# Three PSUM copies of a feed-forward stage go from the vector engine to ScalarE, and a tanh recurrence is dealt out anew

## The reference, cut to what matters

```
# layer 0, feed-forward
h = bit_linear(x, w1)                      # 256 -> 1024, quantized x and ternary weights
h = silu(depthwise_conv1d(h, conv_w, 3 taps) + conv_b)
h = bit_linear(h, w2)                      # 1024 -> 256: max over a token, scale, round, multiply
# layer 1, recurrence, 1024 steps that depend on each other
Bu = x @ B_w.T + B_b
state = tanh(state * exp(A) + Bu[:, t])    # 64 states, 4 sequences
y = states @ C_w.T + C_b + (x @ D_w.T + D_b)
```

## Time and profile before

| | us |
|---|---|
| median of 3 runs (2614.31 to 2617.99) | 2614.32 |
| the profiled execution, its own time | 2614.64 |
| its span, first to last instruction | 2612.9 |
| `ffn0`: first silu to last silu, 31 slots | 1135.75 to 1558.86 |
| `ffn0` with steps: from silu of slot 7 to the last | 1213.17 to 1558.86 |
| `keys` stage | 1591.4 to 1659.1 |
| `values` stage | 1659.9 to 1731.3 |
| `cross_layer1` | 1731.9 to 2189.3 |

### The profile page before, as it was taken

One profiled execution on the slowest core, in us unless ns is written; L12 is line 12 of the kernel. 1 busy time (PEld: TensorE's weight loads), 2 busy tenths in 40 slices (PEclk: granted clock), 3 DMA queues, 4 the chain that ended last, 5 costly groups with the idle time before them and its releaser, 6 DMA issues. The chain is left out here.

```text
span 2612.9 us, 35515 instructions
## 1 busy us (share of the span) xinstructions
PE 1856.3 (71%) x11685; PEld 1177.5 (45%) x11696; DVE 1883.8 (72%) x4634; ACT 1337.4 (51%) x3303; POOL 802.5 (31%) x889
## 2 busy tenths in 40 slices
PE   8759999999478888844554446668999995444444
PEld 4413333333267767733443333345667773222222
DVE  4678888884478888868888883335666664888886
ACT  2106666667033334415999998977742221233332
POOL 3500000000054364323333320004435533444442
PEclk9959999999599999967666765678999997666665
DMA  2011111110200000000000001000000000000000
GB/s 71 16 32 27 31 29 30 30 28 7 55 13 11 29 11 11 3 1 1 1 1 1 1 1 51 13 17 1 17 1 1 1 1 30 7 13 11 10 13 15
DMA packets 42805, 41.50 MB, mean 16 GB/s; under 512 B 16054, under 2 KB 34670, under 8 KB 42622
## 3 DMA queue, kind: packets, MB, share of 16 engines
q1 hardware_dynamic: 42622, 39.23, 5.6%
HBM read 22.03 MB, written 4.19 MB: 10 GB/s over the span
## 5 line engine op out<-in xcount | busy, mean ns | idle before, releaser
L763 ACT ACTIVATE ST<-ST,aexp 128x1 f32<-128x1 f32 x2046 | 574.7, 374 | 11.6 <-PEq L57 11.6
L597 ACT ACTIVATE PT<-PS 128x512 f32<-128x512 f32 x576 | 309.8, 597 | 219.4 <-PE PS L482 188.5
L94 PE MATMUL PS<-ident,j_t 128*128 128x128 f32 x320 | 84.9, 431 | 233.9 <-DVE j_t L155 156.7
L558 DVE CUSTOM_DVE_ANT_0 junk<-PS,maskw 128x128 bf16<-128x128 f32 (+3 forms) x512 | 226.5, 486 | 33.8 <-PE PS L459 33.8
L459 PE MATMUL PS<-KT,QT 48*128 48x512 bf16 (+3 forms) x768 | 190.4, 351 | 54.1 <-DMA QT<-QS 33.0
L94 PE MATMUL PS<-ident,X 128*128 128x128 f32 x320 | 76.2, 325 | 212.6 <-DVE X L128 195.3
L561 DVE TENSOR_REDUCE MX<-PS 128x1 f32<-128x512 f32 x256 | 164.6, 685 | 27.7 <-PE PS L459 24.8
L501 PE MATMUL PS<-PT,VP 128*32 128x256 f32 (+1 forms) x2560 | 184.2, 370 | 0.0
L94 PEld LDWEIGHTS PS<-ident,j_t 128*128 128x128 f32 x320 | 59.4, 219 | 259.2 <-DVE j_t L155 169.0
L123 POOL TENSOR_TENSOR n_rs<-n_ve,neghalf 128x1 f32<-128x1 f32 x96 | 110.3, 1165 | 208.0 <-DVE n_ve L118 208.0
L1561 PE MATMUL PS<-L_xattn_VW,l_pT 112*128 112x256 f32 x704 | 161.4, 385 | 9.1 <-DVE i_xb L1587 6.3
(11 more groups left out here) (297 smaller groups left out, 4471.0 us busy)
## 6 DMA issues: line engine op xcount, KB each, us to landing
KT<-KS SPq DMA_DIRECT2D x192, 32.0 KB, 2.0
QT<-QS SPq DMA_DIRECT2D x192, 32.0 KB, 2.0
xs<-in_x SPq DMA_DIRECT2D x8, 512.0 KB
cx<-in_x SPq DMA_DIRECT2D x32, 128.0 KB, 2.0
out<-j_xn SPq DMA_DIRECT2D x32, 128.0 KB, 1.7
QT<-NMT SPq DMA_DIRECT2D x192, 2.0 KB
f_raw<-in_L_ffn_w SPq DMA_DIRECT2D x2, 1024.0 KB, 5.4
j_raw<-in_L_ffn_w SPq DMA_DIRECT2D x2, 1024.0 KB, 5.1
```

Of the source, the lines that this page charges most:

```text
L94: last = T.transpose(dst[:, i * P:(i + 1) * P], src[:, i * P:(i + 1) * P], idm[:, :])
L558: V.tensor_tensor_reduce(junk[u % 3][:, 0:w * P], bank(u % 3)[:, 0:w * P], maskw[:, BANK - w * P:], 1.0, NEG, ALU.add, ALU.max, MX[i % 2][ ...
L597: C.activation(PT[n % 4][:, 2 * pr + e, 0:w], bank(3 + u % 3)[:, 0:w], ACT.Exp, scale=0.25).then_inc(e_done, 1)
L763: C.activation(self.ST[:, m, t:t + 1], self.ST[:, m, t - 1:t] if t else self.zero[:, :], ACT.Tanh, bias=self.BU[:, m, t:t + 1], scale=self ...
```

## The change

In `ffn0_and_recurrence` DVE loses its three operations on PSUM and ACT gets them, as `copy`, `copy` and an Identity activation with the bias. The steps of a slot go from 22 to 16, in four pieces of 2, 6, 4 and 4 with the new operations and silu between them. DVE gets a wait on its own `f_ds`. `keys` and `values` get 90 steps each and not 110; `cross_layer1` 14 a slot and not 12, in four pieces (3, 5, 3, 3).

```diff
@@ keys() and values(), act()
-                self.act_more(110)
+                self.act_more(90)
@@ ffn0_and_recurrence, dve()
-                if on(d):
-                    V.wait_ge(f_hqtr, d + 1)
-                    if d >= 2:
-                        V.wait_ge(f_mm2, d - 1)
-                    V.tensor_copy(hqT[d % 2][:, :], bank(6).bitcast(BF16)).then_inc(f_hqT, 1)
...
                     V.wait_ge(f_mm2, d + 1)
+                    V.wait_ge(f_ds, d + 1)
...
-                if on(d):
-                    V.wait_ge(f_xtr, d + 1)
-                    V.tensor_copy(xT[d % 2][:, :], bank(3)[:, 0:D]).then_inc(f_xT, 1)
...
-                if on(d):
-                    V.wait_ge(f_bmm, d + 1)
-                    V.tensor_scalar(R.BU[...], bank(3)[rows(d), D:D + P],
-                                    R.bb[rows(d), :], None, ALU.add).then_inc(R.fed, 1)
@@ ffn0_and_recurrence, act()
-                b = j - 1
+                b, d = j - 1, j - 3
                 if j >= 7:
-                    R.act_states(11)
+                    R.act_states(2)
+                if on(d):
+                    C.wait_ge(f_hqtr, d + 1)
+                    if d >= 2:
+                        C.wait_ge(f_mm2, d - 1)
+                    C.copy(hqT[d % 2][:, :], bank(6).bitcast(BF16)).then_inc(f_hqT, 1)
+                if j >= 7:
+                    R.act_states(6)
                 if on(b):
                     C.wait_ge(f_cR, b + 1)
                     C.activation(g[b % 2][:, :, :], g[b % 2][:, :, :], ACT.Silu).then_inc(f_silu, 1)
                 if j >= 7:
-                    R.act_states(11)
+                    R.act_states(4)
+                if on(d):
+                    C.wait_ge(f_xtr, d + 1)
+                    C.copy(xT[d % 2][:, :], bank(3)[:, 0:D]).then_inc(f_xT, 1)
+                if j >= 7:
+                    R.act_states(4)
+                if on(d):
+                    C.wait_ge(f_bmm, d + 1)
+                    C.activation(R.BU[...], bank(3)[rows(d), D:D + P],
+                                 ACT.Identity, bias=R.bb[rows(d), :], scale=1.0).then_inc(R.fed, 1)
@@ cross_layer1, act()
-                R.act_states(6)
+                R.act_states(3)
                 if on(c):
...
+                R.act_states(5)
                 if on(f):
...
-                R.act_states(6)
+                R.act_states(3)
                 if on(sc):
...
+                R.act_states(3)
                 if on(p):
```

More of the change, by code:

```diff
@@ L1439, in dve @@
                     qF.dve_round(c, hq[c % 2][:, :], tmp[c % 2][:, :]).then_inc(f_hq, 1)
-                if on(d):
-                    V.wait_ge(f_bmm, d + 1)
-                    V.tensor_scalar(R.BU[rows(d), (d % B) // 2, (d // B) * P:(d // B) * P + P], bank(3)[rows(d), D:D + P],
-                                    R.bb[rows(d), :], None, ALU.add).then_inc(R.fed, 1)
                 if on(a):
@@ L1462, in act @@
                 if j >= 7:
-                    R.act_states(11)
+                    R.act_states(4)
[6 more added lines that the diff above has]
+                    C.wait_ge(f_bmm, d + 1)
+                    C.activation(R.BU[rows(d), (d % B) // 2, (d // B) * P:(d // B) * P + P], bank(3)[rows(d), D:D + P],
+                                 ACT.Identity, bias=R.bb[rows(d), :], scale=1.0).then_inc(R.fed, 1)
         def pool():
```

## The result

The changed kernel took 2623.06 us (median of 7 runs, 2620.49 to 2627.12), the kernel before 2614.31 us on the same chip (7 runs, 2613.75 to 2617.99). The ratio is 1.0032, with a 95% interval of 1.0020 to 1.0044: slower by 0.3%. The profiled execution of the changed kernel was the fastest of its seven, 2620.49 us, against 2614.64 for the profiled one of before.

The account below looks back on a forecast made before the run. DVE with POOL was taken to close the feed-forward slot, and ACT's list order after the change. The terms 32.3 - 4.8 - 4.8 - 11.1 - 5.2 gave +6.4 us on 2614.64, so 2621.0, range 2607 to 2635.

Parts of the forecast that it names:

- its step for the slots: `cross_layer1`: `i_xT` comes 1.67 us earlier, PE fills the slot, 0.93 less in each of 8 slots, -7.4 us.
- the one for the opening: `cross_layer1`: two ACT-bound slots get 4 more activations, 1.1 us each, +2.2; if the opening gains too, the stage's bound is -9.
- The chain of the slot: Feed-forward: silu, 10 steps, `f_xT`, addition, `f_hqT` at 7.07 us, second matmul, `f_y`, taps, then silu at 15.12.
- Its length: Feed-forward slot with steps: 15.12 us against 13.83, +1.29 each, +32.3 us for 25 slots.
- The matmul's clock: Feed-forward, second matmul: 1.05 us at 2.4 GHz to 1.92 at 1.2 GHz; the median 1.37 was taken.
- Rivals 2 and 3: Feed-forward: cheap copy or fast PE, 2605 to 2613 us, chance 0.12; second matmul staying at 1.2 GHz, 2635, chance 0.12.
- Slots before the recurrence: Feed-forward, four slots without steps: DVE's loop decides, 1.2 us less each, -4.8.
- The stage's end: Feed-forward, behind the last silu's start: 26.8 us in place of 31.65, -4.8.
- keys: `keys`: 40 activations fewer, -11.1 us, with ACT still ending last.
- values: `values`: no change, as ACT wasn't last; the stage getting longer through its clock would show the forecast wrong.
- cross_layer1: `cross_layer1`: -7.4 us for the slots and +2.2 for the opening, -5.2 in all, bounds 0 and -9.
- Rival 4: `cross_layer1` does not become PE's: 12 more slots with steps pay 0.93 us each, +11 + 2, 2639 us; chance 0.06.

Follow-up runs that it names:

- Experiments 1 and 2: Changed kernel, steps moved on ACT: two from ahead of `f_hqT` to behind it, 2593.58 us; all but four behind it, 2555.85 us.
- experiment 7: Changed kernel with `f_hqT` alone back on DVE and the two steps ahead of it joined to the six: 2592.23 us, 0.9910 of the kernel before.
- experiment 6: Changed kernel with eleven idle transposes on PE ahead of its wait for `f_xT`, from slot 8 on: 2616.12 us, 1.0004 of the kernel before.
- Experiment 8: Changed kernel with all steps but four behind `f_hqT`, 88 in `keys`, 124 in `values`, none in the first three `cross_layer1` slots: 2534.96 us.
- experiment 4: Changed kernel with `cross_layer1`'s old places (6, 6), 110 steps in `keys` and 125 in `values`: 2654.20 us, 1.0147 of the kernel before.
- experiment 3: Kernel before, copies left on DVE, with 90 steps each in `keys` and `values` and the changed kernel's places in `cross_layer1`: 2594.10 us, ratio 0.9912.
- experiment 5: Changed kernel with the halves of the recurrence's rows exchanged, even tiles in rows 64 to 127: 2623.47 us in one run.

## Why the prediction was right, and where its terms were off

The forecast was 2621.0 us, and 0.57 for slower by over 0.2%. The mechanism that it gave for the feed-forward stage is the one that the runs show. In `cross_layer1` its step for the slots held, and the one for the opening had the wrong sign. By its steps:

- **The chain of the slot.** Right in its order and nearly in every time up to `f_hqT` (7.04 against 7.07), in the copy (1.004 us against 1.01; that the line between a bf16 and an f32 row hits it so closely is in part luck, as no row had tested such a line), in the handoff before `f_y` (0.04 against 0.09) and in the waits. Experiments 1 and 2 show that its place costs, since they move steps and nothing else: 1.12 us moved, 1.20 gained; the rest moved, and DVE with POOL closes the slot.
- **Its length.** 15.29 us and not 15.12, which is +4.2 us over 25 slots. It has two parts. Every second slot has `f_hqT` 0.39 later, which had no term: one price stood for both halves, and on ACT the rows 64 to 127 are dearer. The mean start is 7.22 and not 7.07, +0.15. The second matmul took 1.45 and not 1.37, another 0.08. The shorter handoff and the copy take 0.06 back, and the sum is 15.29, as measured.
- **The matmul's clock.** The two ends of the scatter were as foretold, 1.05 and 1.89 us; the size was in part luck. The prediction gives 1.37 as the median of the 32 slots before. The trace has a median of 1.33 and a mean of 1.43, and a sum over slots needs the mean. Now 13 of the 25 slots have 1.05 and 12 have 1.89, so no slot is like the mean of 1.45. Rivals 2 and 3 were the two ends of this scatter; neither came, as both levels occur in turn: slots of 14.69 beside 15.94 in the first half of the stage, 15.10 beside 15.53 in the second.
- **Slots before the recurrence.** 12.66 us, four times 1.17 less, -4.7 (forecast -4.8).
- **The stage's end.** 27.19 us behind the last silu and not 26.8; before it was 31.65. That is -4.5 (forecast -4.8). With +36.5 for the slots these make +27.3, and +27.2 was measured.
- **keys.** -12.1 and not -11.1. The 40 activations were -11.1 as priced, and another 1.0 us comes from the steps beginning 6.25 and not 7.28 us behind the stage's beginning, as the copy of the context ahead of them is done sooner.
- **values.** +1.0 where I had 0, and this is one of the signs of being wrong that the prediction named: `values` longer through its clock. ACT is not last there, as the forecast said. The first projection takes 21.24 us in both. The second product, four groups of 36 matmuls, takes 34.7 us before and 35.8 after, and that is the difference. Its last group shows why, first before and then after:

```profile
1721.71 8.02 PE L1024 MATMUL PS<-L_xattn_wo,L_xattn_VX 128*112 128x256 f32 x36 [2.45 <-DVE L_xattn_VX L857]
```

```profile
1735.53 9.71 PE L1024 MATMUL PS<-L_xattn_wo,L_xattn_VX 128*112 128x256 f32 x36 [2.45 <-DVE L_xattn_VX L857]
```

  The same matmuls behind the same wait, with a granted clock of 1.00 in the first and 0.82 in the second; the first of the four groups gives 0.6 back (10.64 and 10.01 us). It is small beside the rest, and it doesn't follow from the 90 steps: the runs that have 90 steps here took from 72.4 (experiment 7) to 73.6 us (experiment 6) for the stage. What sets the clock's phase there stays open.
- **cross_layer1.** -9.9 and not -5.2, the largest miss, and in the other direction from the slot's. ACT's `i_xT` is a poor mark for the slots here: the change itself moves it 1.67 us forward within the slot, and it moves again where the steps run out. PE's groups of scores (L1536, after the change L1541) are a steady one. These are the third and fourth of the stage, before and after:

```profile
1784.85 4.38 PE L1536 MATMUL PS<-L_xattn_M,l_xT 128*128 128x512 f32 x12 [0.97 <-DVE l_s L1594]
...
1803.09 4.30 PE L1536 MATMUL PS<-L_xattn_M,l_xT 128*128 128x512 f32 x12
```

```profile
1801.36 4.38 PE L1541 MATMUL PS<-L_xattn_M,l_xT 128*128 128x512 f32 x12 [0.97 <-DVE l_s L1599]
...
1815.96 4.30 PE L1541 MATMUL PS<-L_xattn_M,l_xT 128*128 128x512 f32 x12
```

  From the fourth group to the thirteenth it took 123.0 us before and 115.3 after, -7.7. The term for the slots (-7.4) held: six slots went down by 0.92 or 0.93 each, and three more by 0.7, as they stayed at 13.1 us. The rest of the stage behind them is 0.4 longer. The miss is the opening, from the stage's beginning to the fourth group: 71.8 us before, 69.2 after, -2.6, where I had +2.2 for four more activations in slots that are ACT's alone. The first two of these are indeed longer by 1.1 each (8.05 from `i_xT` to `i_xT` and not 6.93), just as worked out. But the slot between the two groups shown took 18.2 us before and takes 14.6 now. Before, PE waited 2.30 us there for `i_xT`, and its next product with `l_pT` took 6.94 us at a granted clock of 0.72; now the wait is 1.62, and the product takes 4.99 us. The forecast's lower bound of -9 had named this ("if the opening gains too") and was passed by 0.9. Experiment 8 shows that the steps of the opening were costly all along, 21 us.
- **Rival 4** had its price right, as experiment 4 shows, and didn't come, since the new places free PE's way (experiment 3).

The two large misses are near each other in size, +4.5 in the feed-forward stage and -4.7 in `cross_layer1`, and so are the two small ones, -1.0 in `keys` and +1.0 in `values`. So the sum of +6.4 came out at +5.85. That the total is so close is luck; the terms were off by up to 5 us each.

## What to carry to other kernels

An engine with an in-order list has a load and an order, and the order can cost more: with the same instructions a slot was 15.29 or 12.68 us, the whole 0.3% slower or 2.3% faster than before (0.9% of this is the gain of the later stages, which both have). When a copy on which others wait goes to another engine's list, count what stands ahead of it there, from the last thing that engine waited for, and put filler that nothing waits for behind it. And filler that leaves one stage arrives in another, whose own slack at each place decides its price (0 or 0.93 us a slot here, by where in the slot it stands).

## What the runs showed of the hardware

- An activation of 64x128 from rows 64 to 127 of PSUM onto the same rows of `ST` came with 0.39 us more on ACT, before and behind it, than the same one on rows 0 to 63, with its own duration nearly the same (0.36 and 0.35, experiment 5).
- The copy of 128x1024 bf16 out of PSUM takes 1.00 us on ACT and 0.69 on DVE (the changed kernel and experiment 7). For 256 columns of f32 it is 0.35 on ACT in the changed kernel, and 0.41 on DVE.
- Idle transposes on PE made the work behind them faster: the mean granted clock of the slots rose from 0.64 to 0.79 and the stage became 7.1 us shorter (experiment 6).
